# A Newton step moved from VectorE to GpSimd, a variance kept in PSUM, and gate rows spread in four 32-row tiles in two of four slots

## The reference, cut to what matters

```python
# block 1: attention by 1x1 convolutions on LayerNorm over the 64 channels (eps 1e-6)
k = relu(Wk xn + bk); q = relu(Wq xn + bq); v = Wv xn + bv      # 8 heads of 8 channels
context = einsum('bhkn,bhvn->bhkv', k, v)                        # summed over all 16384 pixels
x = x + Wr (einsum('bhkv,bhkn->bhvn', context, q)) + br
# block 2: each pixel is a token of 64 values; 8 experts, the best 2 are used
p = softmax(layernorm(t) @ router_w + router_b); top 2 of p, scaled to sum to 1
t = t + sum over the 2 of  p_e * (layernorm(t) @ expert_w[e] + expert_b[e])
```

## Time and profile before

| what | value |
|---|---|
| median of 3 runs | 662.58 us (661.94 to 663.03) |
| the profiled execution's own time | 661.13 us |
| its span | 659.3 us |
| PE busy | 612.2 us, 93% of the span |
| DVE busy | 506.5 us, 77% |
| ACT busy | 420.3 us, 64% |
| POOL busy | 396.4 us, 60% |
| granted TensorE clock over the span | 0.991 of full speed |

### The profile page before, as it was taken

The page is one execution under the profiler, slowest core; times in us unless marked ns, Lnnn a source line. Parts: engine busy times, 40 slices in busy tenths (PEclk is TensorE's granted clock), DMA queues, the critical chain, the costliest instruction groups (busy, mean ns, idle before and its releaser), DMA issues.

```text
span 659.3 us, 21452 instructions
## 1 busy us (share of the span) xinstructions
PE 612.2 (93%) x8318; PEld 277.4 (42%) x8318; DVE 506.5 (77%) x1176; ACT 420.3 (64%) x800; POOL 396.4 (60%) x350
## 2 busy tenths in 40 slices
PE   3799989779999999999999999999999999999997
PEld 1566656444444444444444444444333333332232
DVE  3434444798888888898888888988798999989954
ACT  2265646576767676766676676775857667676552
POOL 7223252127666566667666566656677767777986
PEclk9999989799999999999999999999999999999999
DMA  6132535395555566655556665544565667545652
GB/s 151 33 100 67 146 100 130 81 226 132 139 131 138 141 158 160 145 134 127 145 129 147 146 162 129 129 120 109 133 150 135 145 159 176 130 96 120 151 132 49
DMA packets 32663, 86.22 MB, mean 131 GB/s; under 512 B 7650, under 2 KB 7826, under 8 KB 32562
## 3 DMA queue, kind: packets, MB, share of 16 engines
q1 hardware_dynamic: 32082, 84.64, 53.4%
q0 software_dynamic: 288, 0.19, 0.2%
q10 hardware_dynamic: 192, 0.01, 0.0%
HBM read 34.47 MB, written 16.78 MB: 78 GB/s over the span
## 4 chain that ended last, share of the span: by engine, by line
PE 72%; DVE 18%; issue 6%; ACT 2%; POOL 2%; DVEq 0%; ACTq 0%; POOLq 0%
PE bank L1103 28%; PE bank L1089 8%; PE bank L1026 6%; PE bank L1004 5%; PE bank L990 5%; DVE z L834 4%; PE bank L949 3%; PE bank L973 3%; PE bank L1050 3%; PE bank L1100 3%; DVE x L734 2%; DVE osb L844 2%; PE bank L1075 2%; DVE xnT L689 2%; DVE bank L749 1%
## 5 line engine op out<-in xcount | busy, mean ns | idle before, releaser
L442 POOL TENSOR_TENSOR z<-gbs,x1d 128x512 f32<-128x512 f32 x256 | 320.6, 1278 | 170.8 <-ACT gbs L579 78.0
L1106 PE MATMUL bank<-z,ew 128*64 128x512 f32 x512 | 244.6, 599 | 0.0
L1103 PE MATMUL bank<-z,ew 128*64 128x512 f32 x512 | 243.6, 598 | 0.0
L579 ACT COPY gbs<-bank 128x512 f32<-128x512 f32 x256 | 140.9, 595 | 46.4 <-PE bank L1089 46.0
L834 DVE TENSOR_TENSOR z<-bank,x1d 128x512 f32<-128x512 f32 x256 | 165.3, 678 | 6.3 <-PE bank L1089 6.3
L433 POOL TENSOR_TENSOR xsq<-xin 128x512 f32<-128x512 f32 x64 | 65.4, 1044 | 85.0 <-DMA xin<-in_x_dram 67.4
L1103 PEld LDWEIGHTS bank<-z,ew 128*64 128x64 f32 x512 | 64.9, 136 | 103.4 <-issue 96.9
L1089 PE MATMUL bank<-grows,sel 64*64 64x512 f16 x1024 | 85.7, 387 | 6.1 <-ACT grows L573 4.8
L503 ACT COPY xn<-bank 128x512 f32<-128x512 f32 x64 | 34.4, 590 | 62.4 <-PE bank L949 62.4
L1106 PEld LDWEIGHTS bank<-z,ew 128*64 128x64 f32 x512 | 64.4, 136 | 1.1 <-POOL z L442 1.1
L734 DVE SCALAR_TENSOR_TENSOR x<-bank,br_col,x_again 128x512 f32<-128x512 f32 x64 | 45.0, 745 | 20.0 <-PE bank L1050 20.0
(11 more groups left out here) (135 smaller groups left out, 819.9 us busy)
## 6 DMA issues: line engine op xcount, KB each, us to landing
x1d<-x SPq DMA_DIRECT2D x128, 256.0 KB, 4.5
xin<-in_x_dram SPq DMA_DIRECT2D x64, 256.0 KB, 4.2
x_again<-in_x_dram SPq DMA_DIRECT2D x64, 256.0 KB, 4.1
out_dram<-osb SPq DMA_DIRECT2D x128, 128.0 KB, 2.6
k<-in_const_dram SPq DMA_DIRECT2D x1, 453.5 KB, 4.0
ew_nat<-in_L_ffn_expert_w_dram POOLq DMA_DIRECT2D x2, 64.0 KB, 6.4
sel<-in_const_sel_dram SPq DMA_DIRECT2D x1, 128.0 KB, 3.3
bk_rows<-bk_wide ACTq DMA_DIRECT2D x6, 1.0 KB, 1.7
```

Of the source, the lines that this page charges most:

```text
L442: pool.tensor_tensor(z[:, 1, i % R_Z, :], gbs[:, i % R_Z, :], x1d[:, g % 2, 1, u * NT:(u + 1) * NT], ALU.mult).then_inc(z_pool, 1)
L579: nc.scalar.copy(gbs[:, i % R_Z, :], bank[:, :]).then_inc(taken_of(("spread", i, 1)), 1)
L1103: pe.matmul(out_bank[0:C, :], ew[:, j, :], z[:, 0, i % R_Z, :], start=False, stop=(j == PAIRS - 1), skip_group_check=True).then_inc(prod_d ...
L1106: pe.matmul(out_bank[C:P, :], ew[:, j, :], z[:, 1, i % R_Z, :], start=False, stop=(j == PAIRS - 1), skip_group_check=True).then_inc(prod_d ...
```

## The change

Three parts are made together.

1. Newton's step for x leaves DVE. POOL does it in four operations on SBUF at the head of slot 3, before the products of that slot. The arithmetic becomes root x root, x variance, x -0.5 + 1.5, x root.
2. The gates' variance is written to bank 7 instead of SBUF, the reciprocal reads it there, and Newton's first operation multiplies variance by root (one input in PSUM, one in SBUF) instead of root by root (both in SBUF). The count of operations stays.
3. The spreads of the iterations of slots 1 and 2, which are issued in slots 0 and 1, use tiles of 32 rows by 128 columns, one matmul for an iteration and half: even j from `grows`, odd j from a copy of the first 16 rows at 32 partitions further, `grows_again`. SyncE makes the copy with two DMAs a group. The spreads issued in slots 2 and 3 keep the four quarters. `sel` grows by two matrices, and POOL clears `grows_again` at the start.

```diff
+IN_QUARTERS = (0, 3)
+        grows_again = sb("grows_again", [P, 2, NP], F16)
-        N_XSTAT, N_GATE = 7, 27
+        N_XSTAT, N_NEWTON, N_GATE = 4, 4, 27
+            def repeat_gates(g):
+                when_taken(sp, ("gate_rows", g, 0))
...
+                for s in range(S):
+                    sp.dma_start(grows_again[C * s + 32:C * s + 32 + 2 * E, g % 2, :],
+                                 grows[C * s:C * s + 2 * E, g % 2, :]).then_inc(grows_again_in[g % 2], 16)
@@ the loop of SyncE
                     store(n - L_EXPERTS, 0)
+                if real(n - L_TURN_GATES):
+                    repeat_gates(n - L_TURN_GATES)
                 if real(n - L_AGAIN):
                     load_again(n - L_AGAIN)
@@ GpSimd
-            for tile in (w_nat, rw_nat, eb_in):
+            for tile in (w_nat, rw_nat, eb_in, grows_again):
                 pool.memset(tile[:], 0.0).then_inc(cleared, 1)
             pool.wait_ge(cleared, 3)
...
+            def x_newton(g):
+                own, root, work = g * N_NEWTON, xstat[:, 4, :], xstat[:, 5, :]
+                pool.wait_ge(xstat_root, g + 1)
+                pool.tensor_tensor(work, root, root, ALU.mult).then_inc(xstat_pool, 1)
+                pool.wait_ge(xstat_pool, own + 1)
+                pool.tensor_tensor(work, work, xstat[:, 2, :], ALU.mult).then_inc(xstat_pool, 1)
+                pool.wait_ge(xstat_pool, own + 2)
+                pool.tensor_scalar(work, work, -0.5, 1.5, ALU.mult, ALU.add).then_inc(xstat_pool, 1)
+                pool.wait_ge(xstat_pool, own + 3)
+                pool.tensor_tensor(rstd[:, g % 2].rearrange("p u a -> p (u a)"), work, root, ALU.mult
+                                   ).then_inc(xstat_pool, 1)
...
                 for k in range(SLOTS):
+                    if k == 3 and real(n - L_COLS):
+                        x_newton(n - L_COLS)
                     for i in iterations(n, k + 1):
                         product(i)
@@ DVE
             def normalise(g, s):
-                dve.wait_ge(xstat_dve, (g + 1) * N_XSTAT)
+                dve.wait_ge(xstat_pool, (g + 1) * N_NEWTON)
...
-                    lambda: dve.tensor_scalar(bstat[:, 1, :], dev_work[1], 0.0, EPS_FFN, ALU.max, ALU.add),
-                    lambda: dve.reciprocal(bstat[:, 2, :], bstat[:, 1, :]),
-                    rooted, dev[1], dev[2],
+                    lambda: dve.tensor_scalar(dev_work[2], dev_work[1], 0.0, EPS_FFN, ALU.max, ALU.add),
+                    lambda: dve.reciprocal(bstat[:, 2, :], dev_work[2]),
+                    gate_root,
...
-                    if k == 3 and real(n - L_COLS):
-                        x_deviations(n - L_COLS, 4, N_XSTAT)
@@ broadcast, for iterations outside IN_QUARTERS
+                    if u == 0 and j == 3:
+                        pe.wait_ge(grows_again_in[g % 2], 32 * (g // 2 + 1))
+                    source = grows_again if j % 2 else grows
+                    for s in range(S):
+                        use = ("spread", i, s)
+                        bank = when_free(pe, use)
+                        first = C * s + 32 * (j % 2)
+                        pe.matmul(bank[:, :], sel[first:first + 32, j, :], source[first:first + 32, g % 2, columns],
+                                  start=True, stop=True).then_inc(filled_of(use), 1)
```

More of the change, by code:

```diff
@@ L137, in constants @@
     f32 = np.concatenate([eye, centre, same, heads, parts, first, means.reshape(P, 4 * W), bias_rows, both], axis=1)
-    sel = np.zeros((P, PAIRS, P), np.float16)
-    for p in range(PAIRS):
+    sel = np.zeros((P, PAIRS + 2, P), np.float16)
+    for p in range(PAIRS + 2):
+        pair, again = (p, p % 2) if p < PAIRS else (2 * (p - PAIRS) + 1, 0)
         for m in range(P):
-            hit = row_e == 2 * p + m // C
-            sel[hit & (kind == 0), p, m] = 1.0
-            sel[hit & (kind == 1), p, m] = LO
-    return np.ascontiguousarray(f32), sel.reshape(P, PAIRS * P), np.eye(P, dtype=np.float16)
+            hit = row_e == 2 * pair + m // C
+            sel[hit & (kind == 4 * again), p, m] = 1.0
+            sel[hit & (kind == 4 * again + 1), p, m] = LO
+    return np.ascontiguousarray(f32), sel.reshape(P, (PAIRS + 2) * P), np.eye(P, dtype=np.float16)
 def metaformer_block(nc, x, Wk, bk, Wq, bq, Wv, bv, Wr, br, router_w, router_b, expert_w, expert_b,
@@ L236, in metaformer_block @@
         g_own, g_all = g2[:, 0], g2[:, 1]
-        dev_work = [bank[7][:, QG * E + QG * i:QG * E + QG * (i + 1)] for i in range(2)]
+        dev_work = [bank[7][:, QG * E + QG * i:QG * E + QG * (i + 1)] for i in range(3)]
         second_work = bank[7][:, 0:QG]
@@ L253, in metaformer_block @@
         x1d_in = [sem(f"x1d_in{i}") for i in range(2)]
+        grows_again_in = [sem(f"grows_again_in{i}") for i in range(2)]
         stored = [sem(f"stored{i}") for i in range(2)]
@@ L339, in spread @@
                                      ).then_inc(x1d_in[g % 2], 16)
+            def repeat_gates(g):
+                when_taken(sp, ("gate_rows", g, 0))
+                if g == 0:
+                    sp.wait_ge(cleared, 4)
+                if g >= 2:
+                    for s in range(S):
+                        when_taken(sp, ("spread", (g - 1) * U * PAIRS - 1, s))
+                for s in range(S):
+                    sp.dma_start(grows_again[C * s + 32:C * s + 32 + 2 * E, g % 2, :],
+                                 grows[C * s:C * s + 2 * E, g % 2, :]).then_inc(grows_again_in[g % 2], 16)
             def store(g, u):
@@ L651, in then @@
                     dve.wait_ge(set_dve, n_set[0])
-            def newton(out, root, variance, work):
-                return [lambda: dve.scalar_tensor_tensor(work[0], root, -0.5, root, ALU.mult, ALU.mult),
-                        lambda: dve.tensor_tensor(work[1], work[0], variance, ALU.mult),
-                        lambda: dve.scalar_tensor_tensor(out, work[1], 1.5, root, ALU.add, ALU.mult)]
             def halves(a):
@@ L669, in x_deviations @@
                     lambda: dve.tensor_scalar(xstat[:, 2, :], xstat[:, 1, :], 0.0, EPS_CONV, ALU.max, ALU.add),
[L670 to L672 removed]
+                    lambda: dve.reciprocal(xstat[:, 3, :], xstat[:, 2, :])]
                 assert len(steps) == N_XSTAT
@@ L1083, in broadcast @@
                     when_taken(pe, ("gate_rows", g, 0))
-                for s in range(S):
-                    use, rows = ("spread", i, s), slice(C * s, C * s + C)
-                    bank = when_free(pe, use)
-                    for a in range(2):
-                        cols = slice(C * a, C * a + C)
-                        ins = pe.matmul(bank[cols, :], sel[rows, j, cols], grows[rows, g % 2, u * NT:(u + 1) * NT],
-                                        start=True, stop=True)
-                    ins.then_inc(filled_of(use), 1)
+                columns = slice(u * NT, (u + 1) * NT)
+                if i // PER_SLOT % SLOTS in IN_QUARTERS:
+                    for s in range(S):
+                        use = ("spread", i, s)
+                        bank, rows = when_free(pe, use), slice(C * s, C * s + C)
+                        for a in range(2):
+                            cols = slice(C * a, C * a + C)
+                            ins = pe.matmul(bank[cols, :], sel[rows, PAIRS + j // 2 if j % 2 else j, cols], grows[rows, g % 2, columns],
+                                            start=True, stop=True)
+                        ins.then_inc(filled_of(use), 1)
+                else:
+                    if u == 0 and j == 3:
+                        pe.wait_ge(grows_again_in[g % 2], 32 * (g // 2 + 1))
+                    source = grows_again if j % 2 else grows
+                    for s in range(S):
+                        use = ("spread", i, s)
+                        bank = when_free(pe, use)
+                        first = C * s + 32 * (j % 2)
+                        pe.matmul(bank[:, :], sel[first:first + 32, j, :], source[first:first + 32, g % 2, columns],
+                                  start=True, stop=True).then_inc(filled_of(use), 1)
             def experts(i):
```

21 lines of the change are left out of this document (11 added, 10 removed).

## The result

The changed kernel takes **653.14 us** in the median (650.98 to 654.6, four runs) against 662.26 (660.6 to 663.03) for the kernel before on the same chip: a ratio of 0.9863, 95% interval 0.9828 to 0.9898. It is 9.1 us faster, inside the range (640 to 656) and 7.1 us short of the forecast. The profiled execution took 653.81 us, 7.3 less than the 661.13 of before.

What follows compares the result with a forecast made beforehand. PE's work was taken to set most of the time, DVE operations blocked by POOL's products some stretches. From 661.1, -7.8 - 1.0 - 6.3 - 2.1 + 1.0 gives 644.9; with 1.45 to the median, 646 us, range 640 to 656.

Steps and rivals of the forecast that it cites:

- Row tiles, full overlap: PE's spreads in slots 0 and 1: four row tiles run side by side, 0.32 to 0.35 us instead of 0.56.
- The rival of pairs: PE's spreads: row tiles overlap only in pairs, 0.56 us again, spreads give nothing, 654 us; chance 0.15.
- the serial one: PE's spreads: four row tiles run one after another, 64 slots of 0.98 us instead of 0.56, 681 us; chance 0.06.
- the 4 us of doubt: PE's spreads: at the skill's factor 3.07 a spread takes 0.28 us instead of 0.21, sum 4 us poorer.
- Newton's step on POOL costs nothing in full steps: POOL's four operations, 1.5 us (bounds 1.3 and 2.5), fit its 1.64 us idle time between products of slots 2 and 3.
- So the whole loss goes: 5 x 1.55: Long full steps: PE's whole loss of 1.57 us against short ones goes, 7.8 us in all.
- 1 us of reserve: DVE in long full steps: line 749, still with two SBUF inputs, would be late next, with 1 us left.
- Parts 1 and 2 give DVE 2.6 us: DVE in the long full step: Newton's step leaving gives about 1.6 us, variance in the bank 1.0.
- DVE arrives there 0.25 us earlier: Late steps: DVE may catch POOL's product boundary by 0.04 us, saving 1 us in four steps, 642 us; chance 0.2.
- Start +1.0: Kernel start: POOL's clearing of grows_again ahead of the weight loads takes 1.0 to 1.8 us; 1.0 us taken as cost.
- fill -1.0: The same blocked chain at 130 to 145 us, where the pipeline fills, should give 1.0 us.
- the rival in which the stall only moves: DVE: another two-SBUF-input operation (line 749, 667 or 668) is caught each time, the 7.8 us stay, 653 us; chance 0.12.

Runs made afterwards that it cites:

- four other profiles with the same early code: Changed kernel with quarter spreads; quarter spreads and gates' variance in SBUF; gates' variance in SBUF; gates' mean in bank: 655.67, 656.64, 651.02, 647.02 us profiled.
- part 3 alone: Changed kernel with x's Newton step back on DVE and the gates' variance back in SBUF: ratio 1.0181 to the kernel before, 670.46 us profiled.
- parts 1 and 2 in quarters: Changed kernel with every spread in four quarters again, the row copy still made but not read: ratio 0.9930 to the kernel before, 655.67 us profiled.
- parts 1 and 3: Changed kernel with the gates' variance back in SBUF, new spreads kept: ratio 0.9849 to the kernel before, 651.02 us profiled.

## Why the prediction was right, and where it was not

- **Row tiles, full overlap**: right. 0.33 us for 0.56, and 0.10 more in the keys ahead of slot 0's spread (1.17 to 1.27, from the matmul of their bias on), where I had 0.08. Short full steps -0.35, short late -0.26, three of the last steps -0.23 to -0.27 for the 0.21 forecast. The rival of pairs and the serial one fell. By the Trainium skill (TensorE: Matmul & The Clock Gate, Part 3: Packing small matmuls) the factor over one after another is 3.07; here it is about 4 x 0.21 / (0.33 - 0.08) = 3.4, an estimate from the rows, so the 4 us of doubt (64 x 0.07 is 4.5) did not come.
- **Newton's step on POOL costs nothing in full steps**: right; 1.30 us there, and 0.20 to 0.25 an operation on the mean, where 0.30 was taken.
- **"So the whole loss goes: 5 x 1.55"**: this step failed. Long full steps went to 18.15, not 17.6. I held that line 749 would be late next and that 1 us of reserve was left. What PE waited for there was z, behind line 697 (667 before), which stands for POOL's product, and three gate operations; line 667 I had only in a rival, and the gate operations nowhere. They keep 0.56 in each of five steps, 2.8 us, and swallow the gain of the new spreads there. In the steps with a folded context and the two ahead of them the spreads gave nothing either (18.17 to 18.15, 19.02 to 19.2), 1.7 us more; in the two with a folded context it was line 749 after all (776 now), caught for 1.3 us. So full steps brought 8.7 us in 16, where 14.1 had been put on 18.
- **"Parts 1 and 2 give DVE 2.6 us"**: right as a count, wrong as a reason to need both. Either alone frees 1.3 us a pair.
- **"DVE arrives there 0.25 us earlier", the toss of 0.04 us**: the toss was lost by 0.03, since line 776 missed the boundary; and a lost toss is dearer than no change, since a caught operation waits for all of the next product. The long late step is 0.20 us longer (a wait for a whole product in place of most of one), so late steps brought 0.6 and not the 1.25 I had on them. The last five brought 1.8, with 0.56 in one of them from part 2, which I had not seen.
- **Start +1.0 and fill -1.0**: this term was mis-sized most. The profile shows +3.6 where I had 0; the four other profiles with the same early code show +0.8 to +2.3, so part of the 3.6 is this one execution's. The clearing was priced well enough (1.80 us for an upper bound of 1.8, some 0.5 at the first squares). What I passed over is that Newton's step has a wait in POOL's order and that the preparation of biases stands behind it: I looked for POOL's work in early steps, found it idle, and did not ask what it does once. The chain at 130 to 145 us gave no gain that the profiles show.
- **The sum**: -16.2 forecast, -7.3 in the profile, by stretches +3.6, -8.7, -0.6, -1.8 and 0.2 around them. That 653.1 lies in the range of 640 to 656 owes something to the range's width: it is outside the 643 to 650 of the forecast alone, and the pairs, for which the upper end was set, did not come. It is also the number of the rival in which the stall only moves (653), but by a sum of other terms: of the 7.8 us that the rival would keep, 2.8 stayed. (The time of the slower rival adds up to 682, with the 1.0 at the start: 27 - 8.8 + 1.0 = 19.2.) **The direction** held because the forecast's surplus was larger than all that went wrong. It did not have to: part 3 alone, which gives PE the same 0.35 us in short steps, made the kernel 1.8% slower, a case that no rival of mine held.

Why the long full step ends at 18.15 to 18.19 in every mix in which it isn't doubly caught can be read from the traces. Counted from the turning of gates, POOL's pair of products ends at 13.43 to 13.44 us in all of them, the operation behind line 697 starts at 13.49 to 13.53, and the z for PE's queries at 15.28 to 15.32. With parts 1 and 2 in quarters PE is ready for the queries at 15.89 and starts them at 16.01 to 16.02; in the changed kernel it is ready at about 15.57 and starts them at 16.02 as well. With parts 1 and 3 DVE reaches line 697 only at 13.33, its wait is gone, z starts at 15.32 all the same, and PE, 0.56 late from slot 0, no longer waits in slot 2.

Still open: why POOL's pair starts at 10.93 in all of these, and what the long step would take without line 697's wait. I did not try taking its two SBUF inputs away, as no free columns of a bank were at hand for it in that slot.

## What to carry to other kernels

Where one engine's small operations wait for another's whole instruction, the price of an edit is set by phase: a gain of 0.3 us upstream can move the operation to the other side of a boundary and cost 1.1 a step, as part 3 alone did. A wait that you find in a long step may stand in the short one too and cost nothing there: look at both before you call it the cause. List every such operation in the steady step with its distance to the boundary on both sides, and take the shared input away (one operand in PSUM) before shortening anything around it. And when a waiting step is put into an engine's order, look through the fill for work that the engine does once and that now stands behind it.

## What the runs showed of the hardware

- An operation of VectorE with two SBUF inputs waits for the end of GpSimd's running product and so takes up to 1.2 us for 16 columns, where 0.17 is enough (lines 697 and 698); with one input in PSUM it takes 0.18 to 0.20 us beside the same product, and so does one with a single SBUF input. The Trainium skill (SBUF — State Buffer, SBUF: two separate sides) says that such an operation and one of GpSimd's exclude each other for the whole instruction; this case's rows agree, in operations of 16 and 32 columns as well. What I had not expected is that of two such operations in a row each waits for a product of its own when products come back to back, so that the two cost 2.4 us (lines 677 and 678, 697 and 698).
- Four matmuls of 32 rows by 128 columns at 512 moving columns in fp16 run together: 0.33 us from their start to the next matmul's, with the change of tile shape in it.
- GpSimd's operations on 128 x 16 values took 0.20 to 0.25 us on the mean of a line (0.40 the first one in the step shown), with 0.08 between dependent ones; the clearing of 128 x 2048 fp16 values took 1.80 us.
